# The row maxima as the bias of the exponential, one exponential for each head

## The reference

```python
q = proj(hidden_states, Wq, bq) * scaling          # 16 heads of 8; scaling = 8 ** -0.5
k = proj(hidden_states, Wk, bk)
v = proj(hidden_states, Wv, bv)
scores = jnp.einsum('bhsd,bhtd->bhst', q, k)
scores = scores + chunk_attention_mask(S)[None, None]   # 0 or -1e30
probs = jax.nn.softmax(scores, axis=-1)
out = jnp.einsum('bhst,bhtd->bhsd', probs, v)
```

## Time and profile before

| | |
|---|---|
| median of 3 runs | 1640.91 us (1638.66 to 1643.88) |
| the profiled execution | 1642.63 us, span 1640.8 us |
| granted TensorE clock, mean | 0.99 of full speed |
| L965, SiLU of the gate (ACT) | 512 x 598 ns |
| L686, exponential (ACT), and table loads ahead of it | 96 instructions, 90 loads x 1283 ns |
| L747, row maxima (DVE) | 96 instructions |

### The profile page before, as it was taken

The page is one execution under the profiler, slowest core; times in us unless marked ns, Lnnn a source line. Parts: engine busy times, 40 slices in busy tenths (PEclk is TensorE's granted clock), DMA queues, the critical chain, the costliest instruction groups (busy, mean ns, idle before and its releaser), DMA issues. The chain is left out here.

```text
span 1640.8 us, 31286 instructions
## 1 busy us (share of the span) xinstructions
PE 1545.5 (94%) x12484; PEld 1293.3 (79%) x12484; DVE 1021.3 (62%) x2316; ACT 953.3 (58%) x1306; POOL 411.3 (25%) x403
## 2 busy tenths in 40 slices
PE   5399969999999999999999999999999999999998
PEld 2278857788878888787888878887788888887887
DVE  5556638656676667666675676667756665576543
ACT  6273737854678466846666586467744664366421
POOL 5332232322223222133320342123401221122000
PEclk9999989999999999999999999999999999999999
DMA  5000120002001200021000300030002000200000
GB/s 186 13 36 31 53 90 1 36 19 78 8 1 54 80 18 2 12 88 45 8 2 25 116 5 8 2 111 33 1 1 78 8 1 1 78 8 2 1 7 7
DMA packets 40961, 55.48 MB, mean 34 GB/s; under 512 B 2560, under 2 KB 18944, under 8 KB 40816
## 3 DMA queue, kind: packets, MB, share of 16 engines
q1 hardware_dynamic: 40816, 53.48, 9.5%
HBM read 42.75 MB, written 10.72 MB: 33 GB/s over the span
## 5 line engine op out<-in xcount | busy, mean ns | idle before, releaser
L965 ACT ACTIVATE h<-pg 128x512 f32<-128x512 f32 x512 | 304.5, 598 | 569.4 <-PE pg L263 567.2
L909 PE MATMUL pd<-w_down,h 128*128 128x128 f32 x4096 | 537.4, 280 | 0.8 <-DVE x L991 0.8
L909 PEld LDWEIGHTS pd<-w_down,h 128*128 128x128 f32 x4096 | 504.1, 192 | 31.0 <-issue 9.5
L1011 DVE TENSOR_TENSOR h<-h,pu 128x512 f32<-128x512 f32 x512 | 346.4, 679 | 175.0 <-PE pu L263 173.6
L816 POOL TENSOR_TENSOR att_arena<-att_arena 100x500 f32<-100x500 f32 (+2 forms) x192 | 172.9, 900 | 597.1 <-DVE att_arena L747 589.3
L261 PE MATMUL pg<-ffn_x_hi,w_gate_hi 128*128 128x512 f32 x512 | 247.1, 483 | 0.0
L261 PE MATMUL pu<-ffn_x_hi,w_up_hi 128*128 128x512 f32 x512 | 205.8, 402 | 15.4 <-DVE h L1011 15.2
L262 PE MATMUL pu<-ffn_x_lo,w_up_hi 128*128 128x512 f32 x512 | 204.1, 399 | 0.0
L262 PE MATMUL pg<-ffn_x_lo,w_gate_hi 128*128 128x512 f32 x512 | 204.0, 399 | 0.0
L263 PE MATMUL pg<-ffn_x_hi,w_gate_lo 128*128 128x512 f32 x512 | 203.8, 398 | 0.0
L263 PE MATMUL pu<-ffn_x_hi,w_up_lo 128*128 128x512 f32 x512 | 203.7, 398 | 0.0
(11 more groups left out here) (170 smaller groups left out, 1758.6 us busy)
## 6 DMA issues: line engine op xcount, KB each, us to landing
arena<-bc_spread SPq DMA_DIRECT2D x56, 256.0 KB
qk_rows<-qk_parts SPq DMA_DIRECT2D x32, 256.0 KB, 2.3
q<-qk_rows SPq DMA_DIRECT2D x32, 256.0 KB, 3.7
k<-qk_rows SPq DMA_DIRECT2D x32, 256.0 KB, 4.4
arena<-in_x SPq DMA_DIRECT2D x8, 256.0 KB, 2.8
x<-in_x SPq DMA_DIRECT2D x8, 256.0 KB, 3.1
h<-in_w_gate SPq DMA_DIRECT2D x8, 256.0 KB, 6.5
h<-in_w_up SPq DMA_DIRECT2D x8, 256.0 KB, 2.7
```

The source lines that it names most:

```text
L909: last = nc.tensor.matmul(pd[:, t * P:(t + 1) * P], h_b[:, d % NH, t * P:(t + 1) * P], wd[:, d % NCH, :], start=d % CPE == 0 and t == 0, s ...
L965: nc.scalar.activation(h_b[:, c % NH, :], pg[c % 2][:, :], ACT.Silu).then_inc(gate_done, 1)
L1011: nc.vector.tensor_tensor(h, h, pu[d % 2][:, :], ALU.mult).then_inc(h_done, 1)
```

## The change

The row maxima are no longer subtracted from the scores. VectorE multiplies them by -(8 ** -0.5) into `nmax` (two buffers, 8 columns each), right behind the maximum and waiting for it, and ScalarE gives that column to the exponential as its per-partition bias: exp(scale * s - scale * max). A bias holds one value for each partition, so each head needs an instruction of its own. The semaphore `s_sub` now comes from VectorE's multiply; GpSimd takes no part in the softmax any more.

```diff
-        att_ar = sb("att_arena", [P, N_S + N_V + L + 2 * QT + 8])
+        att_ar = sb("att_arena", [P, N_S + N_V + L + 2 * QT + 24])
...
+        nmax = [att_ar[:, o1 + 8 + 8 * s:o1 + 16 + 8 * s] for s in range(2)]
...
                     act.wait_ge(s_sub, NUNIT * j + n + 1)
-                    u = s_u[n % 2][0:nq, :, :, 0:nk]
-                    nc.scalar.activation(u, u, ACT.Exp, scale=float(HD) ** -0.5).then_inc(s_exp, 1)
+                    for h in range(8):
+                        u = s_u[n % 2][0:nq, h // 4, h % 4, 0:nk]
+                        last = nc.scalar.activation(u, u, ACT.Exp, scale=float(HD) ** -0.5,
+                                                    bias=nmax[n % 2][0:nq, h:h + 1])
+                    last.then_inc(s_exp, 1)
...
-                    if n >= 1:
+                    if j or n:
                         dve.wait_ge(s_sub, NUNIT * j + n)
                     nc.vector.reduce_max(smax[0:nq, :, :], s_u[n % 2][0:nq, :, :, 0:nk], AX).then_inc(s_max, 1)
+                    dve.wait_ge(s_max, NUNIT * j + n + 1)
+                    nc.vector.tensor_scalar(nmax[n % 2][0:nq, :], smax[0:nq, :, :].rearrange("p r g -> p (r g)"),
+                                            -float(HD) ** -0.5, None, ALU.mult).then_inc(s_sub, 1)
...
-                for n in range(NUNIT):
-                    i, p = UNITS[n]
-                    nq, nk, _, _ = size(i)
-                    yield Att.at(j, n + 2 / 3)
-                    pool.wait_ge(s_max, NUNIT * j + n + 1)
-                    for rr in range(2):
-                        u = s_u[n % 2][0:nq, rr, :, 0:nk]
-                        ins = nc.gpsimd.tensor_tensor(u, u, smax[0:nq, rr, :].unsqueeze(2).broadcast_to([nq, 4, nk]),
-                                                      ALU.subtract)
-                        if rr == 0:
-                            link(ins)
-                        else:
-                            ins.then_inc(s_sub, 1)
```

## The result

The changed kernel takes 1655.77 us (median of 5 runs, 1653.71 to 1657.07) against 1643.27 us before (1638.66 to 1644.30): a ratio of 1.0082, 95% interval 1.0065 to 1.0100. It is slower by 12.5 us by the medians (13.5 by the ratio); 1661 was forecast. The profiled execution took 1657.07 us, span 1655.3 us.

The account below looks back on a forecast made before the run. TensorE, busy 94% of the span, was taken to bound the kernel; others count only where it waits. 15.2 (ScalarE) + 3 (VectorE) + 4 (clock) - 2 (GpSimd) = +20 us, about 1661 us, own range 1648 to 1676.

Parts of the forecast that it names:

- VectorE's multiply: VectorE's small multiply and two waits: 0.3 us a unit, 29 us of VectorE, +3 us at TensorE.
- GpSimd's removal: GpSimd's subtraction goes, 172.9 us off an engine TensorE never waits for: credited 2 us, bounds 0 and 12.5.
- A unit's addition: ScalarE's eight exponentials in place of one: 2.55 us instead of 1.04 a large unit, +1.51 us; +145 us over 96 units.
- rival A: No overlap between the small exponentials on ScalarE: +2.4 us a unit, about +46, 1687 us; chance 0.12.
- The walk over the units: Timeline walk of ScalarE's lateness reaching TensorE: 13 units lose, 8.6 us in attention 0, 6.6 in attentions 1 to 7, +15.2.
- The first place: Attention 0 at 271.59: L655 starts 0.54 us after the copies' first half ends, so 1.0 us is lost.
- The place at 497 us: Two SiLUs at 497.11 last till 498.19, gate matmul starts at 498.62; two units' additions meet, delay arriving 2.6 us.
- the last place: At 1431.44, 0.70 us behind its exponential: a loss of 0.9 us.
- The clock: Two or three of the 13 new TensorE pauses bring the lower clock: +4 us, bounds 0 and 15.
- B: Hidden: TensorE's queue gives way, or a step of 0.2 us a head; under 5 us, 1643; chance 0.18.
- C: Faster: pointer free at 0.17 us a head, GpSimd's removal decides; -7 us, 1634; chance 0.08.
- The signs named beforehand: ScalarE busy 1085 to 1110 us, GpSimd 238, VectorE +15 to +25, TensorE's ScalarE waits 15 or more, mostly 262 to 350.

Follow-up runs that it names:

- the eight alone: The kernel before with eight exponentials a unit, bias a fixed column of zeros, GpSimd still subtracting, no VectorE multiply: 1659.6 us, 1.0106 of the kernel before.
- one exponential: The changed kernel with one row maximum over all eight heads and a single exponential with that column as bias: 1640.3 us, 0.9988 of the kernel before.
- the three kernels timed side by side: Eight exponentials alone in the kernel before, 1659.6 us; changed kernel with GpSimd's subtraction kept behind VectorE's multiply and one ScalarE wait, 1662.7; changed kernel again, 1656.2.
- The kernel without the pointer: The changed kernel with the bias left out of the eight exponentials, maxima computed but not used: 1643.7 us, 1.0013 of the kernel before.

## Why the prediction was right

**The direction and the engine.** Slower, through ScalarE's added time, was right: the eight alone cost 16.8 us, and GpSimd's removal and the multiply with one exponential cost nothing.

**A unit's addition.** Forecast 1.51 us, measured 1.39. Both halves were near: 0.387 us a head for 0.40, a step of 0.292 for 0.31. The operand's 0.09 us and the overlap of the earlier trace rows held, and rival A (no overlap, 1687 us) fell with them. A pointer costs 0.387 - 0.296 = 0.09 us (100x125 here and in the kernel without it). The page "ScalarE: Activation LUTs" of the Trainium skill, in its section on what a table load costs, has 93 ns for the pointer and 93 ns of overlap. Both agree with these rows, 0.09 and 0.095 us.

**What reaches TensorE.** The walk over the units gave 15.2 us and the clock another 4: 19 together, where the eight alone measured 16.8. The walk's parts were less exact than its sum.

- Attention 0 was to lose 8.6 us and lost 9.5, of which 1.7 are the low clock at 296 us, so 7.8 by the walk's own account.
- The first place was misread: L655 waits for both copies, and the second ends at 271.45, 0.14 us before it; the row itself shows TensorE idle for 0.17 us there. There was no 0.54 us of room, and the place lost 1.4 us (its wait grew from 0.17 to 1.55) and not 1.0. At 306.93 the forecast 1.0 is what was lost.
- Attentions 1 to 7 were to lose 6.6 us and lost 4.6 net, with wins between. The place at 497 us was foreseen, with 2.6 us; 2.3 were lost between 493 and 500 us, but not by a gate matmul that waits for a SiLU: 1.0 by the scores' longer wait through VectorE, shown above, the rest with the low clock at 505 us. That way isn't in the prediction's list of what reaches TensorE. Near the last place, 0.8 us of the foreseen 0.9 were lost.

That the loss bends was right in kind: the walk had +0.5 us for 0.4 us a unit and 38 for 2.4, and measured were 2 at 0.65 and 32 at 2.15.

**The clock.** Two or three new pauses were to bring the lower clock. The windows around the four stretches of the changed kernel between 262 and 1545 us:

```profile
296.00:300.00 4.00, 3.76 (x42) 3.45 (x43) 2.20 (x5) 3.94 (x7) 0.00 (x0) 0.57 0.12 44
504.00:508.00 4.00, 4.00 (x16) 3.42 (x16) 3.96 (x10) 3.97 (x9) 0.00 (x0) 0.57 0.17 63
705.00:713.00 8.00, 8.00 (x65) 5.90 (x64) 4.43 (x14) 6.52 (x16) 0.00 (x0) 0.57 0.31 94
883.00:887.00 4.00, 4.00 (x17) 3.48 (x17) 1.30 (x4) 3.96 (x11) 0.00 (x0) 0.57 0.00 0
```

At 0.57 of the clock, 20 us cost 0.43 x 20 = 8.6 us. The kernel before has two such stretches, that of the earlier trace rows and this one, 1.6 and 1.7 us:

```profile
869.00:873.00 4.00, 4.00 (x19) 3.60 (x17) 0.85 (x2) 2.20 (x3) 0.00 (x0) 0.57 0.00 0
```

So the clock costs about 5 us more, for 4 forecast. That the slow stretches follow pauses of TensorE is seen; how much of the loss goes when they go wasn't tried.

**The terms that were off.** The forecast was 20 us, and 12.5 to 13.4 were measured, inside its own range. In the three kernels timed side by side, ScalarE's part with its clock is 16.8 us, 2.4 below the forecast; the other two parts together are -3.4, where 3 - 2 = +1 was forecast. So most of the error lies in these two.

*GpSimd's removal* was credited with 2 us, with the reason that the waits it ends or shortens are not TensorE's own. It is worth 3.4 to 6.6, inside its bounds of 0 and 12.5. A wait ahead of the exponential is room that ScalarE can't use: it stands still there with its table loaded, and the eight come behind it. In the two units that waited longest the removal takes 2.4 us from ScalarE's queue, where the change adds 1.39. The rows show this place by place; that such places make up all of the gain wasn't tried apart. VectorE's wait for GpSimd's product in the scan, which the prediction also named, fell only from 17.6 to 14.0 us. With one exponential the same removal and the multiply together show 2 us at most; the parts don't simply add.

*VectorE's multiply* was put at 0.3 us a unit and 3 us at TensorE. The instruction takes 0.19 us, and its cost lies between 0 and 3.1, not told apart. Its own line, shortest, median and longest in ns:

```profile
L754 DVE TENSOR_SCALAR att_arena<-att_arena x96: 157/171/1159, 234.7 to 1533.4; 100x8 f32<-100x8 f32 x80, 12x8 f32<-12x8 f32 x16
```

By the Trainium skill's page "SBUF — State Buffer", section "Who interferes with whom", the long ones would be those that met GpSimd. The trace agrees: only five of the 96 take more than 0.18 us (0.31, 0.33, 0.33, 0.35 and 1.16), each began while a GpSimd instruction ran, and each ended 0.03 us behind that one's end. The prediction had estimated 9 meetings and counted nothing for them; that was right.

**Rivals B and C.** Hidden (1643 us) and faster (1634 us) were both tied to about 0.2 us a head. The kernel without the pointer has a step of 0.20 us a head and lands at 1643.7, so B's condition and price were right, and the change doesn't meet the condition. C's gain of 7 us didn't come even there.

**The signs named beforehand.** GpSimd's 238 us, TensorE's 17.2 us of waits for ScalarE and two more stretches at the low clock came. ScalarE's 1080.5 us lie just under the 1085 to 1110, VectorE's 11 more under the 15 to 25, and about half of the 17.2 us lie before 350 us, not most.

## What to carry to other kernels

Work moved off an idle engine onto one that is 70% busy costs little as long as it fits the room behind each instruction that somebody waits for, and more for each further microsecond once it doesn't; so list that room place by place before reading the busy shares, and follow a late engine through the others as well, as here through VectorE. Ask of a wait that a change removes whether the engine could have used that time: a wait in front of the work that grows was worth more here than the 2 us credited, though less than its length (3.4 to 6.6 of 12.5 us). And where only a row constant is subtracted, one constant for all heads keeps the single instruction and drops the other engine too, if the heads' scores aren't too far apart.

## What the runs showed of the hardware

- A second wait ahead of the exponential put the 1.28 us table load behind a wait: ScalarE then waited 38.8 us on ACT_TABLE_LOAD where it had waited 14.9 on the exponential, and the kernel lost about 8 us. After adding a semaphore wait in front of an activation, look at where its table load went.
- A per-partition operand costs 0.09 us in each instruction, also in a run of small ones: 0.296, 0.387 and 0.484 us for 100x125 with none, one and two. Neighbours in such a run overlap by 0.095 us.
